# Weights loaded two units ahead, a chunk split earlier, a loop cut in two, and a layer norm by quarters, in a graph layer and mixture-of-experts kernel

## The reference

```
h   = layernorm(x)                                  # x is 2048 x 256
out = (adj / rowsum(adj)) @ h @ W_neigh.T + b_neigh + h @ W_self.T + b_self
x   = x + relu(out)                                 # adj is 2048 x 2048
z   = layernorm(x)
p   = softmax(z @ Wg + bg); the two largest of 8, divided by their sum -> combine
h_e = relu(z @ W1[e] + b1[e])                       # 256 -> 1024
x   = x + sum_e combine[:, e] * (h_e @ W2[e] + b2[e])
```

## Time and profile before

| | us |
|---|---|
| median of 3 runs | 422.39 (421.44 to 422.97) |
| the profiled execution | 421.99 |
| its span | 420.2 |
| TensorE busy | 375.6 |
| VectorE busy | 290.1 |
| ScalarE busy | 230.6 |
| GpSimd busy | 114.5 |

### The profile page before, as it was taken

The page is one execution under the profiler, slowest core; times in us unless marked ns, Lnnn a source line. Parts: engine busy times, 40 slices in busy tenths (PEclk is TensorE's granted clock), DMA queues, the critical chain, the costliest instruction groups (busy, mean ns, idle before and its releaser), DMA issues.

```text
span 420.2 us, 9657 instructions
## 1 busy us (share of the span) xinstructions
PE 375.6 (89%) x2942; PEld 365.3 (87%) x2942; DVE 290.1 (69%) x770; ACT 230.6 (55%) x519; POOL 114.5 (27%) x119
## 2 busy tenths in 40 slices
PE   0499899999999989899999999999999999697850
PEld 0377799999999989899999999999999999597850
DVE  4677877888888978996876766666666765645640
ACT  1233543544445557736866776666666775466540
POOL 4000000435454434413333322223333324021120
PEclk9999999999999999999999999999999999759565
DMA  8850155757566274384695756756675644566520
GB/s 260 340 202 0 44 182 204 247 185 257 168 244 234 96 239 141 100 253 82 164 263 136 194 144 178 175 138 150 149 183 130 177 114 77 200 219 179 171 63 5
DMA packets 36701, 70.26 MB, mean 167 GB/s; under 512 B 6080, under 2 KB 26944, under 8 KB 34624
## 3 DMA queue, kind: packets, MB, share of 16 engines
q1 hardware_dynamic: 29952, 61.45, 45.9%
q0 software_dynamic: 6720, 8.46, 11.4%
HBM read 54.02 MB, written 16.40 MB: 168 GB/s over the span
## 4 chain that ended last, share of the span: by engine, by line
PE 74%; DVE 10%; DMA 6%; ACT 3%; issue 3%; SPq 1%; POOL 0%; ACTq 0%; DVEq 0%; POOLq 0%
PE bank L1034 29%; PE both L1068 7%; PE both L1171 7%; PE both L1070 7%; PE both L1069 6%; PE both L1173 6%; PE both L1172 6%; DMA w_raw<-w 3%; DVE split L914 2%; DMA y_c<-ws_t 2%; PE bank L1113 2%; PE bank L1087 1%; DMA zg<-rows 1%; DVE h_lo L942 1%; DVE split L716 1%
## 5 line engine op out<-in xcount | busy, mean ns | idle before, releaser
L459 POOL DMA_INDIRECT out<-y_c,kept x36 | 59.2, 1644 | 109.0 <-issue 80.1
L1171 PE MATMUL both<-split,h_hi 128*128 128x256 f32 x288 | 85.0, 295 | 0.8 <-DVE h_lo L942 0.6
L578 ACT ACTIVATE h_raw<-bank,b_sb 128x256 f32<-128x256 f32 (+1 forms) x160 | 67.0, 462 | 31.5 <-PE bank L1034 29.4
L1172 PE MATMUL both<-split,h_hi 128*128 128x256 f32 x288 | 82.4, 286 | 0.0
L1173 PE MATMUL both<-split,h_lo 128*128 128x256 f32 x288 | 82.4, 286 | 0.0
L433 POOL DMA_INDIRECT rows<-zr,slot_i x32 | 45.2, 1412 | 120.3 <-DVE slot_i L783 115.4
L1068 PE MATMUL both<-split 128*128 128x258 f32 x256 | 76.2, 297 | 1.4 <-DVE self_sb L709 1.4
L1034 PE MATMUL bank<-zt,split 128*128 128x256 f32 (+1 forms) x480 | 68.1, 309 | 9.5 <-DVE split L914 7.8
L1034 PEld LDWEIGHTS bank<-zt,split 128*128 128x128 f32 x480 | 66.9, 217 | 10.0 <-issue 8.3
L1070 PE MATMUL both<-split 128*128 128x258 f32 x256 | 72.2, 282 | 0.0
L1069 PE MATMUL both<-split 128*128 128x256 f32 x256 | 72.0, 281 | 0.0
(11 more groups left out here) (154 smaller groups left out, 525.8 us busy)
## 6 DMA issues: line engine op xcount, KB each, us to landing
w_raw<-w SPq DMA_DIRECT2D x52, 512.0 KB, 5.4
adj_raw<-adj_t SPq DMA_DIRECT2D x16, 1024.0 KB, 5.1
rows<-zeros SPq DMA_DIRECT2D x10, 520.0 KB, 4.6
zg<-rows SPq DMA_DIRECT2D x18, 260.0 KB, 4.1
x_sb<-x SPq DMA_DIRECT2D x4, 512.0 KB, 5.9
out<-x SPq DMA_DIRECT2D x16, 128.0 KB, 1.7
b_sb<-b SPq DMA_DIRECT2D x13, 128.0 KB, 3.3
out<-y_c,kept POOLq DMA_INDIRECT x36, 4.0
```

The costliest lines, as they stand in the source:

```text
L459: pool.indirect_dma_start(out, Rows(kept[:, b, j:j + 1], 0), y_c[:, b, j, :], None, bounds_check=N - 1, oob_is_err=False, compute_op=ALU.a ...
L578: act.activation(h_raw[:, q % 2, c * SLOT:c * SLOT + n], source, ACT.Relu, bias=bias).then_inc(hid_relu, 1)
L1171: pe.matmul(o, h_hi[:, c, t], w_hi[:, d], start=(c == 0), stop=False, skip_group_check=True)
L1172: pe.matmul(o, h_hi[:, c, t], w_lo[:, d], start=False, stop=False, skip_group_check=True)
```

## The change

- SyncE's turns load the weights of unit u+2 where they loaded those of u+1. Those of unit 1 are loaded in the last expert's slots. The last turn's second slot loads none.
- Where a slot splits four chunks (the turns, and slot 3), chunk 1 is split ahead of the last ReLU group.
- Each engine's turns are a loop of 3, and behind an `If(turns > 3)` a loop of the other 11.
- SyncE loads the first quarter of x, the feature weights and the biases, then the other quarters, then the gate's weights.
- The layer norm's scale is made for a quarter of x at a time: the first one up front, the next ones at tiles 1, 5 and 9 of the feature loop. The statistics of tiles 4 to 15 stand between the tiles. ScalarE normalizes (Identity with scale and bias), where VectorE did. The loops of both are written out. `root_of` (ScalarE) waits for the quarter's variances, which `moments` gives with its fourth tile; `norms` (VectorE) waits for the root and makes scale and bias in five linked small operations; `normed` of tiles 4, 8 and 12 waits for `norms`.

```diff
-                with sp.Fori(0, TURNS) as k:
-                    with sp.If(k < turns):
-                        ...
+        def each_turn(eng, turns, turn):
+            with eng.Fori(0, SOON) as k:
+                with eng.If(k < turns):
+                    turn(k)
+            with eng.If(turns > SOON):
+                with eng.Fori(SOON, TURNS) as k:
+                    with eng.If(k < turns):
+                        turn(k)
```

```diff
-                    coming = e + 2 if e + 2 < E else expert(0) if e + 2 == E else None
+                    coming = e + 2 if e + 2 < E else expert(e + 2 - E)
...
+                def turn(k):
+                    for b in range(2):
+                        u = 2 * k + b
+                        hold(y_biased, u + FIXED)
+                        load_biases(1 - b, expert(u + 1))
+                        if b == 0:
+                            coming = expert(u + 2)
+                            load_weights(0, u + E + 2, coming)
+                            load_weights(1, u + E + 2, coming)
+                            rows_free(u + FIXED)
+                            load_rows(b, first_row(u + 2), P)
+                            load_weights(2, u + E + 2, coming)
+                            load_weights(3, u + E + 2, coming)
+                        else:
+                            with sp.If(k + 1 < turns):
+                                coming = expert(u + 2)
+                                for c in range(2):
+                                    load_weights(c, u + E + 2, coming)
+                            rows_free(u + FIXED)
+                            load_rows(b, first_row(u + 2), P)
+                            with sp.If(k + 1 < turns):
+                                coming = expert(u + 2)
+                                for c in range(2, 4):
+                                    load_weights(c, u + E + 2, coming)
```

```diff
                     for c in chunks[0:1]:
                         high_w(1 - v, c, weights_n)
                     for q in range(NQ):
+                        if q == NQ - 1:
+                            for c in chunks[1:-2]:
+                                high_w(1 - v, c, weights_n)
                         relu(s, q, v, n)
...
-                    for c in chunks[1:]:
+                    for c in chunks[1:] if len(chunks) == 2 else chunks[2:]:
                         high_w(1 - v, c, weights_n)
```

```diff
+                normed(0)
+                normed(1)
                 rows_high(0, 0)
-                with act.Fori(0, T // 2 - 1) as k:
-                    for b in range(2):
-                        rows_high(2 * k + b + 1, 1 - b)
-                        features_high(2 * k + b, b)
+                normed(2)
+                for i in range(T - 2):
+                    rows_high(i + 1, 1 - i % 2)
+                    if i in (1, 5, 9):
+                        root_of(i // 4 + 1)
+                    if i + 3 < T:
+                        normed(i + 3)
+                    features_high(i, i % 2)
```

```diff
+                for i in range(T):
+                    if i in (1, 5, 9):
+                        norms(i // 4 + 1)
+                    features(i, i % 2)
+                    if i + 2 < T:
+                        rows_low(i + 2, i % 2)
+                    if i == 0:
+                        moments(6)
+                        moments(7)
+                    elif i <= T // 2:
+                        moments(i + T // 2 - 1)
```

More of the change, by code:

```diff
@@ L468, in _, with turn @@
                     add(s, s % 2, (s + 1) // 2 + 1, past[:, s + 1:s + 2, :] if s < FIXED - 1 else past_u[:, 0:1, :])
[L469 to L473, removed]
+                def turn(k):
+                    for b in range(2):
+                        u = 2 * k + b
+                        add(u + FIXED, b, k + b + FIXED // 2 + 1, past_u[:, bass.ds(u + 1, 1), :], 1)
+                each_turn(pool, turns, turn)
             @block.scalar
@@ L648, in _, with turn @@
                 turns = turns_of(act)
[L649 to L653, removed]
+                def turn(k):
+                    for b in range(2):
+                        slot(2 * k + b + FIXED, b, b, k + FIXED // 2 + 1, k + E // 2 + 1, (0, 1, 2, 3), 2 * k + b + E + 2, P)
+                    results(2 * k + FIXED + 1, 1, 1)
+                each_turn(act, turns, turn)
             @block.vector
@@ L693, in _, with moments @@
-                dve.wait_ge(bias_in, 64)
-                link(dve.tensor_tensor(bias[:], bias_n[:], bias_s[:], ALU.add))
-                def rows_low(i, b, more=True):
+                def moments(t):
+                    if t % 4 == 0:
+                        dve.wait_ge(x_in[t // 4], 16)
+                    link(dve.bn_stats(stats[:, t, :], x_sb[:, t, :]))
+                    last = dve.bn_aggr(mv[:, t, :], stats[:, t, :])
+                    if t % 4 == 3:
+                        link(last)
+                        q = slice(t - 3, t + 1)
+                        dve.tensor_scalar(ln[:, 0, q], mv[:, q, 1], EPS, None, ALU.add).then_inc(var_all, 1)
@@ L698, in rows_low @@
+                def rows_low(i, b):
                     dve.wait_ge(ht_hi, i + 1)
@@ L1012, in _, with turn @@
                 turns = turns_of(dve)
-                with dve.Fori(0, TURNS) as k:
-                    with dve.If(k < turns):
-                        for b in range(2):
-                            slot(2 * k + b + FIXED, b, b, (0, 1, 2, 3), 2 * k + b + E + 1, tab_f[:, 0, bass.ds(2 * k + b, 1)], P)
+                def turn(k):
+                    for b in range(2):
+                        slot(2 * k + b + FIXED, b, b, (0, 1, 2, 3), 2 * k + b + E + 1, tab_f[:, 0, bass.ds(2 * k + b, 1)], P)
+                each_turn(dve, turns, turn)
             @block.tensor
@@ L1233, in _, with turn @@
                 turns = turns_of(pe)
-                with pe.Fori(0, TURNS) as k:
-                    with pe.If(k < turns):
-                        for b in range(2):
-                            slot(2 * k + b + FIXED, b, b, 2 * k + b + E, k + b + FIXED // 2 + 1, P)
+                def turn(k):
+                    for b in range(2):
+                        slot(2 * k + b + FIXED, b, b, 2 * k + b + E, k + b + FIXED // 2 + 1, P)
+                each_turn(pe, turns, turn)
 def kernel(x, adj, L0_gnn_W_neigh, L0_gnn_b_neigh, L0_gnn_W_self, L0_gnn_b_self, L0_ffn_Wg, L0_ffn_bg,
```

107 lines of the change are left out of this document (51 added, 56 removed).

## The result

The changed kernel takes **399.0 us**, median of 4 runs (398.73 to 402.12), against 422.68 of the kernel before in the same session (4 runs); the ratio is 0.945 (0.940 to 0.950). Forecast were 399.4 us and 395.0 to 405.5. The profiled execution took 402.12 us with a span of 400.4; its mean clock is 0.978, while the three other runs have spans of 397.0 to 397.5 and 0.986 or 0.987. The ratios leave out runs more than 1.5% above the fastest of the same kernel, which only one experiment, e8_chunk_rows, had (two of six).

What follows compares the result with a forecast made beforehand. TensorE's own work was taken as the bound, with holes at start and end. Turns -16.6, loops -5.8 and start -0.6 summed to -23.0 from 421.99, giving 399.0, by the median 399.4 us; range 395 to 405.5.

Steps and rivals of the forecast that it cites:

- the start: First stage: features start 6.7 us sooner, faster tiles give 1.1, serial chains at tiles 1, 5, 9 cost 7.2; -0.6 us.
- Turns, -16.6: Last four slots: weights two units ahead remove both stalls, VectorE's order sets the pace, last output DMA moves to 390.6.
- rival E: Features and last four slots: short stalls bring the clock down everywhere, +13.8 us, 436 us; chance 0.03.
- Chunk and loads elsewhere, 0: Slot 3's earlier chunk 1 split and unit 1's loads in the last expert's slots: 0, at most +0.5 for the chunk.
- Two loops, -5.8: Program's end: GpSimd skips 11 unused turns, DRAIN's 5.6 us start when the last DMA's issue ends; -5.8 us.
- D: Features: new stalls at tiles 5 and 9 bring one stretch at 1.2 GHz, 6.2 us, giving 405.6 us; chance 0.10.
- B: First stage: the quarters overlap with the feature tiles, the start keeps 4.4 us, 395.6 us; chance 0.12.
- C: Last slots still fed late, or DRAIN waits for the landing: two to five us more, 401.5 to 404.5; chance 0.20.
- F: Turns: something else keeps each slot waiting as long, only 6.4 us go, 416 us; chance 0.05.
- The signs that I had named: Wrong if ScalarE waits for `w_raw` in last slots, DRAIN exceeds 6 us, aggregation at 44 or 51, clock 0.5 before 380.
- Two GpSimd rounds: Program's end, a sign for right: two GpSimd rounds over unused turns gone to one.

Runs made afterwards that it cites:

- e8_chunk_rows: The changed kernel with chunk 1 split behind the last ReLU group again and SyncE loading the rows ahead of chunk 1; 401.3 us, ratio 0.950.
- e9: The changed kernel with SyncE's old loads, a unit's weights asked for one unit ahead; 420.50 us, ratio 0.997.
- e3: The changed kernel with one loop of 14 turns on each engine again; 405.05 us, ratio 0.958.
- e10: The changed kernel with the first loop cut from 3 to 2 turns, so GpSimd walks through no unused turn; 399.79 us, ratio 0.945.
- e1: The changed kernel with the first stage (loads, layer norm, feature loops) of the kernel before; 399.96 us, ratio 0.947.
- e5: The changed kernel with TensorE's feature loop written out and 18 spare transposes at each of tiles 2, 6 and 10; 398.63 us, ratio 0.943.
- e4: The changed kernel with chunk 1 split behind the last ReLU group again, in the turns and slot 3; 400.88 us, ratio 0.949.
- e6: The changed kernel with TensorE's feature loop written out, no spare transposes; 400.37 us, ratio 0.947.
- e2: The kernel before with only the change's first stage; 423.14 us, ratio 0.999.
- e7: The changed kernel with x loaded before biases, second quarter's scale before the feature loop, later scales ending tiles 4 and 8, users one tile later; 391.93 us, ratio 0.930.

## Why the prediction was right

The number lies well inside the range and close to the forecast. The two large terms were right by their mechanism; the small one, the start, was right by luck.

*Turns, -16.6.* Measured -16.9 in the profiled executions. The stalls went with the late loads (e9), and the pace that I had derived from VectorE's order (9.5, 9.05, 9.5, 9.5) came out as 9.50, 9.23, 9.50 and 9.08, 37.3 us together against 37.6. The output bias ended about 1.2 us after TensorE, as said. The clock stayed at full, so rival E's place in the slots was empty.

*Chunk and loads elsewhere, 0.* From the first aggregation to slot 16 it took 0.4 us less. What I left out is that the chunk's new place and the loads belong together: without the loads it costs 3 to 5 us (by subtraction, e9: 60.5 us from slot 16 to the last output DMA against 57.35, and 420.5 us against 422.2 less 1.0 for the start and 6.05 for the loops). The sum did not hang on it, but who takes over one edit alone would lose by it.

*Two loops, -5.8.* Measured -5.6 in the profiles, 6.05 by e3. The choice of where the DRAIN's 5.6 us begin is shown by e3 and e10. By the figure of the Trainium skill (Advanced Engine Details and Errata, Control Flow Timing) the term would have been 2.4, an estimate.

*The start, -0.6.* The size was right for the wrong balance. By medians it is about -1.0 (e1 against the change), in the profiled execution +3.1. First matmul at 10.56 (I had 10.6); late tiles 4.2, 3.9 and 3.9 us instead of 1.7 (I had 4.2 for tiles 5 and 9); other tiles 1.62 to 1.70 where the clock is full (I had 1.68). The forecast was a start of the aggregation at 48.0; in executions whose clock stayed up it was 46.9 to 47.1 (e5, e8, e9), mainly since late tiles took 3.9 and not 4.2. So the steps were some 1.1 us too dear, and what they lacked is the clock, which in most of the profiled executions takes that back and more: each slow stretch adds about 1.6 us, and the start of the aggregation follows their number:

| slow stretches in the features | aggregation starts at, us |
|---|---|
| 0 (e5, e8, e9) | 46.87, 47.08, 46.91 |
| 1 (e4) | 48.78 |
| 2 (e3, e6; e2, whose features start 1.0 us later) | 50.15, 50.23; 51.10 |
| 3 (the change, e10) | 51.66, 51.78 |

*The rivals.* D's mechanism was there, in small: I priced one stretch at 6.2 us, after the 13.7 us long ones of the earlier trace rows, and gave it 0.10. In the features it comes up to three times an execution and is 3.4 us long, so it costs 1.6, about the same share of its length as there. The profile of the change has three; the other runs, 3.2 us faster at a higher mean clock, would have about one, but they have no trace, so this is argued. B, that the quarters overlap, was not in this kernel, but e7 shows what it is worth if they do: 7.1 us together with the clock that stays up, where I gave the overlap 3.8. C needs late landings: one of 1.0 us was left, and it shows in no slot's length. E's point, short stalls that bring the clock down in the slots, did not come in the change, but e8 has it, with 1.1 us. The Trainium skill (TensorE: Matmul & The Clock Gate, A second HAM failure mode) tells of short idles between groups of matmuls that make the clock swing. The rows here agree in part: the clock fell behind waits of 0.9 to 1.2 us in the features and of 1.1 us in e8, and in other executions stayed up behind the same waits. I had given too little weight to that because the earlier trace rows showed 1.6 us without harm. F is refuted by the slots' starts.

*The signs that I had named.* Of those for a wrong prediction four stand in this profile: ScalarE waited for `w_raw` once in the last slots (1.0 us), the DRAIN is longer than 6 us (6.46), the aggregation starts at 51.66, and the clock is 0.50 before 380 us. The first shows in no slot's length (e7, with a wait of 0.8 us, has the same slots to 0.01 us). The second was ill chosen, since 5.6 us behind the end of a 1.56 us issue make a record over 6 us when the DRAIN starts inside that issue. The last two are one thing, the clock in the features, and are a real miss of the mechanism, which costs about 1.6 us a stretch. "Two GpSimd rounds" among the signs for right is a slip: the earlier trace rows has twelve, and one is left.

## What to carry to other kernels

A stall of the tensor engine can be paid twice, once while it waits and once at the lower clock behind it, so price a long one with its shadow, and look first for loads that are asked for one unit too late. Moving a step ahead on an engine's queue pays only when its input is early enough: the same reordering gave 1.3 us in the last slots with loads two units ahead and made the stall longer with loads one unit ahead. A preparation cut into pieces gained here only where each piece was finished before the steady loop needed it, with the pieces at the end of an iteration and their users one iteration later (e7). Count each loop turn that does nothing, 0.6 us here.

## What was unexpected of the hardware

- The clock fell behind stalls far under the 4.0 us of the earlier trace rows: in the features with two waits of about 1 us shortly ahead of it (28.65 and 30.05, fall at 31.1), and in e8 with none over 1.1 us. It also stayed up through 1.6 us in a busy stretch, and through 2.4 us in e9 where 2.3 us in e5 brought it down. The same first stage shows it or not: e8's and e9's executions had no fall in the features, e10's three. The length of the single wait does not decide, and what does is left open.
- A slow stretch was 3.4 us in the features, 6.8 at 151 us in e5, 10.2 in e8, 13.7 or 17.1 behind the long stalls.
- GpSimd's DRAIN ends 5.6 us after the issue of the last indirect DMA has ended, or 5.6 us after its own start if that is later; the change, e10 and e3 agree to 0.1 us.
- Two small broadcast loads and the feature weights ahead of the second quarter of x made it land at 12.3 us, where behind the first quarter alone it landed at 5.8; in the changed kernel VectorE waited 0.92 us for it. Most of that is the broadcast loads: in e7, where only the feature weights stand ahead of it, it landed at 8.2. While the broadcasts were under way the DMA engines were busy and moved little (share 0.93, 118 GB/s, against 388 at a share of 1.01 in the earlier trace rows):

```profile
5.20:9.20 4.00, 0.33 (x2) 0.29 (x2) 3.45 (x13) 2.22 (x4) 0.00 (x0) 1.00 0.93 118
```
